# A decoder layer with self attention, cross attention and experts on one core: where the next rows are split, which engine normalises the last two x1, and when the expert lists are loaded

## The reference

```python
# self attention, 16 heads of 32
xn = layer_norm(x, in_ln_w, in_ln_b)
q, k, v, p, y = split(xn @ W_in.T + b_in)          # y: 16 forget gates
k = (1 - smear) * k + smear * k_prev
mask = causal - (pos_i - pos_j)                    # pos = cumsum(sigmoid(y))
o = softmax(q k / (s s sqrt(32)) + mask) v
x1 = layernorm(x + layer_norm(silu(p) * o @ W_out.T, out_ln_w, out_ln_b))
# cross attention: the layer's other input gives keys and values beside x1's own
x2 = layernorm(x1 + xattn(ctx, x1, mask))
# 8 experts of 256 -> 1024 -> 256, the best two per row
out = layernorm(x2 + sum of gate * (gelu(x2 W1 + b1) W2 + b2) over the two experts)
```

## Time and profile before

| | us |
|---|---|
| median of 3 runs (2623.00 to 2628.35) | 2625.32 |
| the profiled execution | 2622.04 |
| its span, first to last instruction | 2620.2 |
| TensorE busy | 2354.1 (90%) |
| VectorE busy | 1894.3 (72%) |
| ScalarE busy | 1716.3 (66%) |
| GpSimd busy | 1058.2 (40%) |
| mean granted TensorE clock, share of full | 0.958 |

### The profile page before, as it was taken

How to read it: one execution, slowest core, us unless ns; L and a number is a source line. 1 busy time by engine, 2 the same in 40 slices (tenths; PEclk the granted TensorE clock), 3 DMA queues, 4 the chain that set the end, 5 groups by cost and what they waited for, 6 DMA issues and landing times. The chain is left out here.

```text
span 2620.2 us, 62115 instructions
## 1 busy us (share of the span) xinstructions
PE 2354.1 (90%) x18056; PEld 1969.3 (75%) x18056; DVE 1894.3 (72%) x5304; ACT 1716.3 (66%) x4389; POOL 1058.2 (40%) x1116
## 2 busy tenths in 40 slices
PE   6899999984999999999999999999999479999990
PEld 5777787774777777777777777777776479999990
DVE  6777878774766776677667766776676378888866
ACT  5888878783665666566656665666566256767662
POOL 5555555545333323333333333333332134444434
PEclk9999999996999999999999999999999689999995
DMA  7555555551000000000000000000000367777666
GB/s 197 127 136 132 128 116 128 121 124 38 18 18 3 15 17 17 9 9 17 17 9 9 17 17 9 9 17 17 9 8 9 101 211 243 229 236 237 231 220 201
DMA packets 161045, 224.40 MB, mean 86 GB/s; under 512 B 33920, under 2 KB 127744, under 8 KB 160640
## 3 DMA queue, kind: packets, MB, share of 16 engines
q1 hardware_dynamic: 151008, 202.42, 27.8%
q0 software_dynamic: 9664, 20.53, 2.3%
q10 hardware_dynamic: 224, 0.00, 0.0%
HBM read 140.15 MB, written 24.01 MB: 63 GB/s over the span
## 5 line engine op out<-in xcount | busy, mean ns | idle before, releaser
L1431 ACT COPY x_pt<-x_ptb 128x512 f32<-128x512 f32 x512 | 272.6, 584 | 193.9 <-PE x_ptb L1900 193.3
L1627 DVE CUSTOM_DVE_ANT_0 wox<-x_score,x_mask_add 128x512 f32<-128x512 f32 x352 | 239.3, 683 | 167.3 <-PE x_score L1888 116.2
L1425 ACT ACTIVATE wox<-wox,x_low 128x512 f32<-128x512 f32 x352 | 251.8, 718 | 101.4 <-DVE x_low L1627 98.2
L1328 POOL TENSOR_TENSOR x_k_lo<-x_whole,x_k_hi 128x512 fp32r<-128x512 f32 x128 | 164.4, 1285 | 337.6 <-ACT x_k_hi L1472 335.8
L509 ACT ACTIVATE prob<-prob,low 128x128 f32<-128x128 f32 (+1 forms) x512 | 229.6, 453 | 76.0 <-DVE low L731 74.8
L1917 PE MATMUL x_av<-x_pt,x_vx 128*64 128x256 f32 x2048 | 249.3, 385 | 0.6 <-ACT x_ox_hi L1439 0.6
L1606 DVE COPY x_whole<-x_proj 128x512 f32<-128x512 f32 x192 | 130.7, 687 | 129.1 <-PE x_proj L1818 127.8
L1638 DVE TENSOR_SCALAR wox<-wox,x_rden 128x512 f32<-128x512 f32 x352 | 202.1, 615 | 0.6
L2490 PE MATMUL h_bank<-xg_hi,w_hi 128*128 128x256 f32 x624 | 177.8, 285 | 22.7 <-DVE xg_lo L2363 21.3
L2298 ACT ACTIVATE h_t<-h_bank,b_s 128x256 f32<-128x256 f32 x312 | 131.0, 471 | 102.3 <-PE h_bank L2490 94.8
L1917 PEld LDWEIGHTS x_av<-x_pt,x_vx 128*64 128x64 f32 x2048 | 135.9, 136 | 80.5 <-issue 11.7
(11 more groups left out here) (302 smaller groups left out, 8010.4 us busy)
## 6 DMA issues: line engine op xcount, KB each, us to landing
w_s<-w SPq DMA_DIRECT2D x156, 512.0 KB, 4.7
k_parts<-k_hi SPq DMA_DIRECT2D x128, 128.0 KB, 2.4
q_parts<-q_hi SPq DMA_DIRECT2D x128, 128.0 KB, 2.4
k_parts<-pos_parts SPq DMA_DIRECT2D x128, 64.0 KB, 2.4
k_parts<-k_lo SPq DMA_DIRECT2D x64, 128.0 KB, 2.4
q_parts<-q_lo SPq DMA_DIRECT2D x64, 128.0 KB, 2.4
w_s<-expert_rows SPq DMA_DIRECT2D x16, 512.0 KB, 4.7
b_s<-b SPq DMA_DIRECT2D x39, 128.0 KB
```

What stands on the lines that cost most here:

```text
L1328: pool.tensor_tensor(part_of(n, q_lo, k_lo), whole_of(n), part_of(n, q_hi, k_hi).bitcast(F32), ALU.subtract).then_inc(low_ready.sem, 1)
L1425: nc.scalar.activation(slot, slot, ACT.Exp, bias=low[:, u:u + 1], scale=-1.0, accum_out=den[:, u:u + 1]).then_inc(exp_ready.sem, 1)
L1431: nc.scalar.copy(pt[:, u % PX_RING, :], ptb[u % 2][:, :]).then_inc(pt_taken[u % 2].sem, 1)
L1627: dve.tensor_tensor_reduce(prob_slot(u), score[u % 2][:, :], mask_add[:, :], -X_SCALE, 3.0e38, ALU.add, ALU.min, low[:, u:u + 1]).then_inc ...
```

## The change

Five edits, all within `self_phase` but the last.

1. The high and the low part of the next rows are both made on VectorE, in a new function `split_x`, first thing in step 1 behind the masking; ScalarE's copy and GpSimd's subtraction go.
2. TensorE's `project_y` and k chunk 0 move from step 3 (in front of the transposes) to step 2 (behind them); k chunk 1 moves from step 4 to step 3. Chunks 2 and 3 stay in steps 4 and 5.
3. The x1 of the last two batches is normalised on VectorE, and `out_stats` of the last batch stands in front of the normalising of the one before.
4. The block of `self_phase` ends without GpSimd's drain.
5. In the expert phase's start SP loads the lists in front of w2 of tile 0.

```diff
-        block = stack.enter_context(nc.Block())
+        block = stack.enter_context(nc.Block(no_gpsimd_drain=True))
...
-            def low_x(b):
-
-                pool.wait_ge(xn_hi_ready.sem, xn_hi_ready.at(b, 1))
-                pool.tensor_tensor(xn_lo[:], xn_t[:], xn_hi[:].bitcast(F32), ALU.subtract).then_inc(xn_split.sem, 1)
...
             for b in (B - 1, B):
                 reciprocal_root(b, LN_OUT)
                 residual(b)
-                x1_of(b)
+                reciprocal_root(b, LN_RES)
...
                 taken(ins, XT)
-                act.wait_ge(proj_taken[XT % 2].sem, proj_taken[XT % 2].at(b, XT // 2 + 1))
-                nc.scalar.copy(xn_hi[:], xn_t[:]).then_inc(xn_hi_ready.sem, 1)
...
+            def split_x(b):
+
+                dve.wait_ge(proj_taken[XT % 2].sem, proj_taken[XT % 2].at(b, XT // 2 + 1))
+                dve.tensor_copy(xn_hi[:], xn_t[:]).then_inc(xn_hi_ready.sem, 1)
+                dve.wait_ge(xn_hi_ready.sem, xn_hi_ready.at(b, 1))
+                dve.tensor_tensor(xn_lo[:], xn_t[:], xn_hi[:].bitcast(F32), ALU.subtract).then_inc(xn_split.sem, 1)
...
-                     1: [lambda b: widen(b - 1, 3), lambda b: gate(b - 1, 2)],
+                     1: [split_x, lambda b: widen(b - 1, 3), lambda b: gate(b - 1, 2)],
...
-            for b in (B - 1, B):
-                for part in (out_stats, centred, residual_sum, residual_stats):
-                    part(b)
+            def x1_normalised(b):
+
+                dve.wait_ge(rstd_ready[LN_RES].sem, rstd_ready[LN_RES].at(b, NTH[LN_RES]))
+                dve.wait_ge(x1_stored.sem, x1_stored.at(b, 0))
+                for c in range(TC):
+                    ins = normalise(LN_RES, x1[:, c, :], res1[:, c, :], c)
+                ins.then_inc(x1_ready.sem, 1)
+
+            for part in (out_stats, centred, residual_sum, residual_stats):
+                part(B - 1)
+            out_stats(B)
+            x1_normalised(B - 1)
+            for part in (centred, residual_sum, residual_stats, x1_normalised):
+                part(B)
...
-            split_parts = {3: [inputs[1], k_chunks[0]], 4: k_chunks[1:3], 5: k_chunks[3:], 6: q_chunks[0:2], 7: q_chunks[2:3], 8: q_chunks[3:],
+            split_parts = {3: k_chunks[1:2], 4: k_chunks[2:3], 5: k_chunks[3:], 6: q_chunks[0:2], 7: q_chunks[2:3], 8: q_chunks[3:],
                            12: p_chunks[0:2], 13: p_chunks[2:], 14: v_parts[:1], 15: v_parts[1:]}
-            whole_parts = {9: outputs[:1], 10: outputs[1:], 15: [lambda b: x_transposed(b + 1)]}
+            whole_parts = {2: [inputs[1], k_chunks[0]], 9: outputs[:1], 10: outputs[1:], 15: [lambda b: x_transposed(b + 1)]}
...
                 load_w1(Tile(0, n))
                 load_b1(Tile(0, n))
-                load_w2(Tile(0, n))
                 if n == 0:
                     sp.wait_ge(scattered.sem, scattered.at(B, scattered.per))
                     for k in range(RING):
                         load_tokens(Tile(0, k))
+                load_w2(Tile(0, n))
```

More of the change, by code:

```diff
@@ L444, in _ @@
             pool.memset(pt[:], 0.0).then_inc(consts, 1)
-            low_x(-1)
             pool.memset(prob[:], 0.0).then_inc(consts, 1)
@@ L451, in one_pass @@
             def one_pass(b, more):
-                if more:
-                    low_x(b)
                 reciprocal_root(b - 1, LN_OUT)
@@ L801, in _ @@
             dve.tensor_tensor(win_y_lo[:], win_y[:], win_y_hi[:].bitcast(F32), ALU.subtract).then_inc(consts_v, 1)
+            split_x(-1)
             dve.memset(silu_p, 0.0)
@@ L841, in _ @@
                      15: [lambda b: take_v(b, 0), lambda b: gate(b, 1), lambda b: residual_stats(b - 1)]}
-            last = {**steps, 6: [], 7: steps[7][1:], 10: [], 14: steps[14][:1], 15: steps[15][1:]}
+            last = {**steps, 1: steps[1][1:], 6: [], 7: steps[7][1:], 10: [], 14: steps[14][:1], 15: steps[15][1:]}
             for i in (8, 9, 13):
```

## The result

The changed kernel takes 2612.86 us (median of 5, 2607.66 to 2615.02), the kernel before 2626.55 beside it on the same chip (2623.0 to 2629.48). The ratio is 0.9937, with a 95% interval of 0.9926 to 0.9949: 13.4 to 19.4 us faster. The forecast was 2614, faster. The profiled execution took 2615.02, with a span of 2613.3.

What follows compares the result with a forecast made beforehand. The prediction took the self attention loop to be held by TensorE's waits for ScalarE's copies and by clock falls. Loop -4.5, block's end -4.2 and lists -2.6 made -11.3: 2610.7 on the profiled execution, 2614 as median, range 2609 to 2620.

Steps and rivals of the forecast that it cites:

- The pass at full clock: Self attention loop: a pass without a clock fall goes from 33.59 to 34.4 us, as y is taken later.
- The clock: Self attention loop: fewer clock falls, costing a mean of 0.3 us a pass, so 34.7 against 34.98; -4.5 over 15 passes.
- where 2.67 brought a fall in three of four, I take one in two: Loop steps 1 and 2: TensorE's waits shrink from 2.67 to 2.0 us, so half the passes have a clock fall.
- the forecast's case: Whole kernel: loop -4.5, block's end -4.2, lists -2.6 us, giving 2614; chance 0.45, own range 2609 to 2620.
- the second rival: Loop: the clock falls no more; 34.4 us a pass, -8.7 in the loop, -15.5 in all, 2610; chance 0.20.
- The end of the block: Last two batches of self attention: earlier root saves 2.6, normalising on VectorE 1.6, together -4.2 us; removing the drain 0.
- The lists: Expert phase's start: lists issued ahead of w2 land sooner than their 6.04 us, bringing -2.6.
- nearer the second, since nothing else is in the queue: Expert phase's start: the lists' gain, between 0 and 3.1 us, is taken as 2.6.
- GpSimd's gather and TensorE's first transposes follow directly: Expert phase's start: the gather and first transposes come right behind the lists, so the 2.6 us gain passes on.
- The prologue: Before the loop: splitting the first batch's xn_t on VectorE costs nothing, hidden while waiting for weights; at most 1.2 us uncovered.
- The start of the next block: Behind self attention: the next block starts before 617.23 by 4.2 us plus the loop's gain.
- The slower rival: Loop steps 4 to 6: new waits also drop the clock; 36.1 us a pass, +10 in all, 2635; chance 0.10.

Runs made afterwards that it cites:

- E2: The changed kernel with VectorE's split of the next rows behind widen and gate instead of in front of them: 2606.35 us, ratio 0.9921 to the kernel before.
- E9: The kernel before with TensorE's first products moved to step 2, the split still on ScalarE and GpSimd: 2620.09 us against 2625.62, ratio 0.9978.
- E6: The kernel before with only the last two x1 normalised on VectorE; drain, loop and lists as before: 2616.43 us, ratio 0.9962.
- E3: The changed kernel with w2 of tile 0 issued in front of the expert lists again: 2611.89 us, ratio 0.9937 to the kernel before.
- E8: E2 with w2 of tile 0 issued only once tile 0's gathered rows have landed: 2606.2 us, ratio 0.9918 to the kernel before.
- E5: The kernel before with VectorE's memset of den written as 32 pieces, 31 more instructions ahead of everything: 2617.74 us against 2626.12, ratio 0.9972.
- E1: The kernel before with the loop's part alone (split on VectorE, first products in step 2): 2616.64 us, ratio 0.9953.
- E4: The kernel before with VectorE's memset of den written as ten, nine more instructions ahead of everything: 2628.4 us, ratio 0.9999.

## Why the prediction was right, and where it was right by luck

The call and the time held (2614, measured 2612.86). The steps, one by one:

- **The pass at full clock: right.** 34.4 was forecast, 34.48 came, through the links forecast: the wait of 1.3, the split at 0.50 and 0.69 (0.45 and 0.66), ScalarE's 1.73 for VectorE (1.9), the wait for y of 0.87 (1.0). E2 confirms the cause: with widen and gate ahead of the split the pass is 1.14 shorter, which is more than its whole rise of 0.89.
- **The clock: the step "where 2.67 brought a fall in three of four, I take one in two" was too dark.** Two passes of the twelve have a fall. The mean is 34.55 where I had 34.7: 0.44 a pass below before, 6.5 us in place of 4.5. A fall costs 0.4 where I had 0.6, so all falls come to 0.07 a pass in place of 0.3. That lies midway between the forecast's case and the second rival (34.4, 2610; chance 0.20). I had also named the wrong cause. I argued from the length of the waits; E9 keeps the longest at 1.96 and has a clock of 0.98, E2 cuts it to 1.30 and has 0.97 to 0.98, the changed kernel has 1.30 too and 0.99. By the Trainium skill, "TensorE: Matmul & The Clock Gate" (HAM oscillation), the long single gap is what to avoid. The gaps here are shorter than those that the page speaks of, and the clock falls all the same; the runs show that the longest gap does not decide here. What does, beyond the place of the products, is not settled: pass length and place of work changed together in every kernel I ran.
- **The end of the block: right.** -4.2 forecast, -4.4 in the trace and in E6, and nothing for the drain.
- **The lists: wrong.** The step "nearer the second, since nothing else is in the queue" gave -2.6. The lists did land sooner (the gather starts 3.15 after the first is issued, in place of 7.00), but I stopped at them. Behind them stand the gathered rows, which now share the engines with the w2 that had moved behind the lists. They took 6.67. The step that fails is "GpSimd's gather and TensorE's first transposes follow directly". I had asked whether w2 of tile 0 would be late, not whom it would hold up. Nothing is gained (E3), nor by letting the rows go first (E8).
- **The prologue: right at nothing** as far as seen: the loop's first copy on GpSimd starts at 48.24, before at 48.26.
- **What the forecast did not have: -4.9 in the cross attention.** No step, rival or bound named it. It is shown by E5, which gets it with no edit of substance, and E6 has it without touching the loop.
- **The start of the next block: off.** It was to come 8.7 before 617.23, and comes at 612.45, 4.8 before: in this execution the first pass (+3.5) and the last (+1.7) took back what the thirteen between them gave.

So the sum should have been -6.5 - 4.4 + 0 - 4.9 = -15.8; the measured ratio says -13.4 to -19.4. It takes the mean of twelve passes for all fifteen, and the fifteenth was 33.1 to 33.3 long against 31.6 in all three kernels with the split first (the changed one, E1, E3), which would make it some -14. My -11.3 came near it because a gain that wasn't there (2.6) and one too small (2.0) stood against one that I hadn't seen (4.9).

The slower rival needed the clock to fall behind the new waits of steps 4 to 6 (a pass of 35.43). It did not: the three passes around its two falls, 35.60, 34.93 and 33.75, are together only 0.8 longer than three at full clock.

## What to carry to other kernels

When work moves to another engine, place it in that engine's list where the engine stands waiting for its input, and move the entries behind it in front: here the same instructions in another order took 1.14 us off a pass. When a load is moved ahead of another, follow both to the next transfers that share the engines with them, and ask whether the last to be needed comes any sooner. And before a gain in untouched code is credited to a change, look for stalls that nothing explains: a few instructions more or less on an engine move its instruction loads, and in a long loop that alone was worth 0.2 to 0.3%.

## What the chip did that I had not expected

- A stall that goes with VectorE's instruction loads: 0.36 us of standing per cross pass, with three packets of instructions a pass at places that shift with the number of instructions ahead, and two that don't. 31 more memsets of 128x1 made the kernel 0.28% faster (E5).
- The clock does not follow the longest wait. With equal waits of 0.71 and 1.96, twelve passes had a mean clock of 0.95 with the products in step 3 and 0.98 with them in step 2 (E9); with 0.71 and 1.30, 0.99 in passes of 34.5 and 0.97 to 0.98 in passes of 33.3 (E2). A pass of denser work earned back only 0.4 of its 1.14.
- A gather of 128 rows took 2.74 with little else moving (E8, 96 GB/s in all), 2.95 as the last of a load of weights came in (before, 297 GB/s in its first 1.8 us), and 6.67 where 1 MB of w2 had been issued just ahead of it and w1 of tile 1 followed (after, 295 GB/s).
- The first pass takes 38.0 or 41.3 with the same loop (before, E4): one load of rows that was issued behind 4 MB of weights is used at 63.87 or at 65.83, and the pass begins at 48.26 or 46.57.
